# One transformer layer over 64 images: the small operations of the normalisations with scalars per partition

## The reference, cut to what matters

```python
def _layernorm(x, axis=-1, eps=1e-05):
    m = jnp.mean(x, axis=axis, keepdims=True)
    v = jnp.var(x, axis=axis, keepdims=True)
    return (x - m) / jnp.sqrt(v + eps)
...
    h = _L0_tok_ref(L0_tok_log_dt, L0_tok_Lambda, x, 1024)
    h = h + _L0_attn_ref(_layernorm(h, axis=-1), L0_attn_Wq, L0_attn_Wk, L0_attn_Wv, L0_attn_Wo)
    h = h + _L0_ffn_ref(_layernorm(h, axis=-1), L0_ffn_A, L0_ffn_B, L0_ffn_Wr, L0_ffn_br)
```

## Time and profile before

| | |
|---|---|
| median of 3 runs | 2422.75 us (2420.66 to 2428.7) |
| profiled execution | span 2424.2 us; no other time is listed for it |
| PE busy | 2296.6 us, 95% |
| DVE busy | 1984.5 us, 82% |
| ACT busy | 1829.6 us, 75% |
| POOL busy | 1708.7 us, 70% |
| chain that ended last | PE 74%, DVE 4%, ACT 4%, DMA 2% |
| mean granted PE clock | 0.984 |

### The profile page before, as it was taken

One profiled execution on the slowest core, in us unless ns is written; L12 is line 12 of the kernel. 1 busy time (PEld: TensorE's weight loads), 2 busy tenths in 40 slices (PEclk: granted clock), 3 DMA queues, 4 the chain that ended last, 5 costly groups with the idle time before them and its releaser, 6 DMA issues.

```text
span 2424.2 us, 58812 instructions
## 1 busy us (share of the span) xinstructions
PE 2296.6 (95%) x18704; PEld 1248.9 (52%) x18704; DVE 1984.5 (82%) x7796; ACT 1829.6 (75%) x6270; POOL 1708.7 (70%) x1529
## 2 busy tenths in 40 slices
PE   2999599999999999999999999999999999999986
PEld 2777245555555555555555555555555555555543
DVE  8999468888888888888888888888888888888864
ACT  5988277777777787777778777777877777777763
POOL 1444187777777777777777777777777777777772
PEclk9999799999999999999999999999999999999998
DMA  2888489999999999999999999999999999999985
GB/s 75 260 253 239 111 156 175 187 180 185 189 189 183 191 184 187 182 190 190 184 190 188 187 181 189 191 180 189 190 186 180 189 190 181 190 190 187 180 165 108
DMA packets 1201574, 443.65 MB, mean 183 GB/s; under 512 B 1151600, under 2 KB 1153904, under 8 KB 1201264
## 3 DMA queue, kind: packets, MB, share of 16 engines
q1 hardware_dynamic: 1201264, 439.89, 92.0%
HBM read 87.42 MB, written 67.11 MB: 64 GB/s over the span
## 4 chain that ended last, share of the span: by engine, by line
PE 74%; DVE 4%; ACT 4%; DMA 2%; issue 2%; POOL 1%; SPq 0%; POOLq 0%; ACTq 0%; DVEq 0%
PE pc L876 12%; PE pb L876 11%; PE pa L876 11%; PE pb L862 4%; PE pa L862 4%; PE pb L864 4%; PE pb L863 4%; PE s_ps L889 4%; PE pa L863 4%; PE pa L864 4%; PE pv_ps L904 4%; ACT pr L1024 3%; PE pd L862 1%; PE pd L864 1%; PE pd L863 1%
## 5 line engine op out<-in xcount | busy, mean ns | idle before, releaser
L1024 ACT ACTIVATE pr<-pr,smin 128x128 f32<-128x128 f32 x2048 | 792.6, 388 | 192.1 <-DVE smin L1165 191.9
L1372 POOL TENSOR_TENSOR pr<-pr,rinv 128x512 f32<-128x512 f32 x512 | 576.8, 1137 | 357.8 <-DVE rinv L1173 346.9
L1380 POOL TENSOR_TENSOR p<-pr,p 128x512 f16<-128x512 f32 x512 | 590.0, 1157 | 115.7 <-ACT p L1034 109.3
L1165 DVE CUSTOM_DVE_ANT_0 pr<-s_ps,cst 128x128 f32<-128x128 f32 x2048 | 471.6, 286 | 148.7 <-POOL p L1380 105.9
L1034 ACT ACTIVATE p<-pr 128x512 f16<-128x512 f32 x512 | 319.0, 623 | 171.3 <-POOL pr L1372 148.7
L1024 ACT ACTIVATION_READ_ACCUMULATOR pr<-pr,smin 128x1 f32 x2048 | 382.1, 187 | 0.0
L876 PE MATMUL pa<-wkv_hi,xt 128*128 128x512 f16 x1024 | 327.0, 381 | 23.7 <-DMA xt<-xs 23.7
L876 PE MATMUL pb<-wq_hi,xt 128*128 128x512 f16 x1024 | 327.9, 381 | 0.0
L876 PE MATMUL pc<-wq_hi,xt 128*128 128x512 f16 x1024 | 315.0, 379 | 0.0
L612 PE MATMUL hps<-z,xw 128*128 128x256 f32 x848 | 195.7, 391 | 62.2 <-POOL xw L322 42.2
L612 PEld LDWEIGHTS hps<-z,xw 128*128 128x128 f32 x848 | 164.3, 196 | 93.2 <-POOL xw L322 50.4
(11 more groups left out here) (186 smaller groups left out, 4969.2 us busy)
## 6 DMA issues: line engine op xcount, KB each, us to landing
h<-hout SPq DMA_DIRECT2D x128, 256.0 KB, 3.6
h_ln<-h SPq DMA_DIRECT2D x64, 512.0 KB, 4.2
h_res<-h SPq DMA_DIRECT2D x64, 512.0 KB, 4.5
out<-h SPq DMA_DIRECT2D x64, 512.0 KB, 3.2
pt<-p SPq DMA_TRANSPOSE x512, 3.8
xa<-x SPq DMA_DIRECT2D x16, 256.0 KB, 4.1
xb<-x SPq DMA_DIRECT2D x32, 128.0 KB, 3.8
wst<-wq SPq DMA_DIRECT2D x8, 512.0 KB, 5.8
```

The costliest lines, as they stand in the source:

```text
L1024: last = A.activation(p, p, ACT.Exp, bias=smin[g % 2][:, j:j + 1], scale=-1.0, accum_out=rsum[g % 2][:, j:j + 1])
L1165: V.tensor_tensor_reduce(pr[g % 2][:, cols], s_ps[g % 2][:, cols], mask, 1.0, 3e38, ALU.add, ALU.min, smin[g % 2][:, j:j + 1]).then_inc(ma ...
L1372: nc.gpsimd.tensor_tensor(p3, p3, rinv[g % 2][:, :].unsqueeze(2).broadcast_to([P, HG, P]), ALU.mult).then_inc(p_norm, 1)
L1380: nc.gpsimd.tensor_tensor(p[:, HG * P:], pr[g % 2][:, :], p[:, 0:HG * P], ALU.subtract).then_inc(pl_done, 1)
```

## The change

Three of the four operations of `norm_refine` get another form. The factors that came in as tensors of one column (the second y of y * v * y, the c of y * c, and the scale of mean * -1 * scale) come in as scalars per partition, read by a pointer to one column. The values are the same, and so are semaphores and order.

```diff
@@ -1195,13 +1195,13 @@
                     v, y, a, c, scale, shift = (nrm[w][:, n:n + 1] for n in (0, 2, 3, 4, 5, 6))
                     reached(dve, ln_y[w], 2, b, 2)
-                    V.scalar_tensor_tensor(a, y, v, y, ALU.mult, ALU.mult).then_inc(ln_v[w], 1)
+                    V.tensor_scalar(a, y, v, y, ALU.mult, ALU.mult).then_inc(ln_v[w], 1)
                     reached(dve, ln_v[w], 8, b, 5)
                     V.tensor_scalar(c, a, -0.5, 1.5, ALU.mult, ALU.add).then_inc(ln_v[w], 1)
                     reached(dve, ln_v[w], 8, b, 6)
-                    V.tensor_tensor(scale, y, c, ALU.mult).then_inc(ln_v[w], 1)
+                    V.tensor_scalar(scale, y, c, None, ALU.mult).then_inc(ln_v[w], 1)
                     reached(dve, ln_v[w], 8, b, 7)
-                    V.scalar_tensor_tensor(shift, mv[w][:, 0:1], -1.0, scale, ALU.mult, ALU.mult).then_inc(ln_v[w], 1)
+                    V.tensor_scalar(shift, mv[w][:, 0:1], scale, -1.0, ALU.mult, ALU.mult).then_inc(ln_v[w], 1)
```

## The result

| | before | changed |
|---|---|---|
| median of 4 runs | 2423.72 us (2420.66 to 2428.7) | 2401.68 us (2399.3 to 2402.71) |
| ratio, 95% interval | | 0.9904 (0.9892 to 0.9916) |
| span of the profiled execution | 2424.2 us | 2400.3 us |

The change makes the kernel 22.0 us, 0.96%, faster. 2404.8 us was forecast, with a range of 2398 to 2420. The median before counts one run more than the one of 2422.75 that the forecast was measured from.

A forecast was written before the change was run, and what follows sets the result against it. TensorE nearly bounds the kernel, losing up to 0.36 us per image to waits on a chain headed by the normalisation block. 16.5 steady + 1.8 end - 0.3 pointers = 18.0 us off the median 2422.75, taken as 2404.8 us; range 2398 to 2420.

The forecast's parts named there:

- The removed waits: L1198, L1202 and L1204: 0.23 us each with the new forms, without waiting for GpSimd; 105 us of VectorE time removed.
- rival 2: In the three changed lines: the new forms wait for GpSimd too; +1 us, 2424 us; chance 0.08.
- VectorE's total: Busy time of VectorE over the whole run, expected near 1880 us after the change.
- The move in the image: Second normalisation's block ends 1.79 us earlier; TensorE's scores become the next limit, and all behind comes some 0.65 us earlier.
- The stall of 0.2 us: TensorE's matmul into pb waits some 0.2 us for the q rotation; it goes with over 0.4 to spare.
- The steady sum: 59 images between 400.48 and 2326.95 us: of 21.4 us excess, 2 left aside, 85% of the rest taken, 16.5 us.
- The ends: Last chain through the block, L1198 to L1204: 2.76 us becomes 0.96, 1.8 us less.
- The 0.15 us twice for the pointers: Very first and very last normalisation, with GpSimd idle: each 0.15 us longer, 0.3 us together.
- The sum: Whole kernel: 16.5 + 1.8 - 0.3 = 18.0 us faster.
- rival 1: Steady part: waits vanish but others replace them, cadence hardly changes; 7.5 us gained, 2415 us; chance 0.14.
- rival 3: Low half of xn (L1221) now starts inside a GpSimd operation and collides; +13 us, 2436 us; chance 0.08.

The follow-up runs named there:

- the added delays: Changed kernel with four, seven or ten one-column operations ahead of L1198 in the second normalisation: 2402.64, 2407.19 and 2435.52 us.

## Why the prediction was right

- **The removed waits.** The three lines fell from 634 + 513 + 361 = 1508 ns to 269 + 214 + 215 = 698, 104 us over 128 runs, 105 were forecast. The new forms cost 0.27 us with two pointers and 0.21 with one, where I had taken 0.23 for each; so "at most 0.26" was a little low. That they don't wait for GpSimd (rival 2 had a chance of 0.08) is shown. What the means over 128 runs hid: nearly all of the waiting was in the second normalisation.
- **VectorE's total** was to be near 1880 us and is 1906. The missing term is L1310: the small operation next in the list ran into the GpSimd operation that the three no longer waited for, (828 - 372) ns x 64 = 29 us. I had its row, its eight columns and its place in the list, and did not ask what it would meet.
- **The move in the image.** 1.79 us earlier at the end of the block was forecast, and 1.79 came. Then TensorE's scores were to be the next limit, and they are. The stall of 0.2 us was to go with over 0.4 to spare. The rotation now ends 0.57 us ahead of the matmul, and the added delays show that 1.32 us in all could be given back and 1.88 not. The stall itself was set too small: 0.2 us came from the waits that the profile names, and the images became 0.36 us shorter.
- **The steady sum** was the mis-sized term: 16.5 us, and it is 21.0. I had set aside 2 us for gaps of another cause and 15% for new small waits. There are hardly any: one image of 59 is not at 32.29. Nearly all of the excess of before came from that one chain; with the block of w = 1 alone changed it went as well (32.30 us per image).
- **The ends.** 1.8 us less was forecast where the chain passes through the block near the end. The chain that ended last, in order of time (start us, us, what), answers to rows 11:

```profile
2329.73 0.28 DVE nrm L1198
2330.03 0.17 DVE nrm L1200
2330.22 0.23 DVE nrm L1202
2330.47 0.23 DVE nrm L1204
```

From 2329.73 to 2330.70 us, 0.97 in place of 2.76. The stretch after the 60th transpose shrank by 1.6 us; two profiles of the changed kernel differ by 0.8 in it (95.7 and 94.9), two of the kernel without L1310 by 1.8 (97.3 and 95.5). So it fits the forecast and doesn't show it, apart from the chain above. The 0.15 us twice for the pointers is too small to be seen.
- **The sum** 18.0 us against 22.0 by the medians; the measured time lies inside the range. The start, 1.3 us shorter, was in no term of the sum, and the two profiles of the changed kernel differ by more than that in it (399.15 and 395.68).
- **Rivals.** Nothing took the place of the waits in the cadence (rival 1). The forms do what they say (rival 2); at two columns rival 2 is what happens, and worse. The low half of xn (rival 3) has the mean it had, 904 ns:

```profile
L1221 DVE TENSOR_TENSOR xs<-xn,xs 128x512 f16<-128x512 f32 x128 | 115.6, 904 | 4.4 <-ACT xs L1069 4.4
```

## What to carry to other kernels

A small operation whose mean is two or three times its shortest time is waiting, and its end beside the other engine's end tells for what. Removing such a wait is worth what the chain behind it needs, no more: here the steady part needed less than 0.5 us of the 1.8 (1.32 could be given back for next to nothing), either part of the edit did nearly as well as the whole, and the wait that stays moves to the next operation in the list. A mean over all runs of a line can mix a place where it waits with one where it doesn't; look at the places apart before you size the saving. Here nearly all excess of TensorE over its best cycle hung on one chain, and the discount for new small waits was what the forecast had wrong; the wait that did come anew stood on the next line of the list.

## What the runs showed of the hardware that was not expected

- A tensor_scalar with immediates, SBUF to SBUF in float32, waits for a running GpSimd tensor_tensor at two and three columns (up to 1144 and 1166 ns), one with a pointer and an immediate at eight (L1310, up to 1165 ns). At one column neither does (153 to 155 ns and 212 to 216 ns in 128 runs each). Two columns cost 0.016 us more than one when nothing is in the way (170 and 154 ns), and up to 1 us when something is.
- Pointer scalars cost 60 ns for one and 118 for two over immediates at one column (214, 272 and 154 ns).
